# The LoRA-B products of the gate and up tiles, moved from behind the fourth chunk of x to behind the second and third

## The chip, the cores and the metric

The kernel runs on one core of a Trainium2 chip. The metric is the device time of one execution in microseconds (us). The core's engines are named as in the profile: PE (TensorE, matrix products), PEld (its weight loads), DVE (VectorE), ACT (ScalarE), POOL (GpSimd) and SP (SyncE, which issues most transfers). They run side by side and wait for one another on semaphores.

## The reference

Two residual layers on 8 x 128 tokens of 512 features. The first begins with a gated feed-forward block whose three weight matrices each have a low-rank correction (LoRA, rank 16), chosen for each batch by an index:

```
def lora_add(base, inp, A, B):
    t = einsum('bri,bni->bnr', A[idx], inp)
    return base + einsum('bor,bnr->bno', B[idx], t) * 0.5
gate = lora_add(x @ W_gate.T, x, A_gate, B_gate)      # 512 -> 1376
up   = lora_add(x @ W_up.T,   x, A_up,   B_up)
act  = silu(gate) * up
down = lora_add(act @ W_down.T, act, A_down, B_down)  # 1376 -> 512
```

A linear layer with eight averaged adapters follows and is added to x. The second layer is a linear layer with a batch's own sign matrix, then a mixture of 64 experts of rank 16, of which each token uses 16. All is float32. Only the products for `gate` and `up` are touched by the change.

## The kernel before

Each float32 operand is held as two parts, high and low, whose sum is the number to more digits than the PE takes in one pass. A product is made in three passes (`mm3`, lines 1150 to 1152: high by high, high by low, low by high). The x half is the moving operand, 512 tokens wide (`halves(s)`), and the weights are loaded into the array, 128 by 128.

The 1376 features of gate and up are cut into FT = 11 tiles of 128. Tiles 0, 1 and the last are done ahead, in code written out by hand. Tiles 2 to 9 run in a loop of four rounds with two tiles each (`pe.Fori`, line 1278). A tile is two halves of the tokens (s = 0, 1), and each half fills two banks of PSUM, one for gate (m = 0) and one for up (m = 1). So the loop fills 8 x 2 x 2 = 32 banks. For one bank the PE does:

- `project` (line 1157): for each of the four chunks of x (k = 0 to 3) three passes, 12 products of 512 columns;
- `adapt` (line 1168): two products of 256 columns that add the LoRA-B correction, one for each pair of batches (h = 0, 1). Their weights are `b_st`, 96 rows by 128 columns; the moving operand is `t_st`, 96 rows by 256 columns. The second one raises `gate_ready` or `up_ready`.

`b_st` holds the chosen B rows of the tile. POOL fetches them by an indirect transfer (line 416), ACT writes the high parts for all 96 rows (`b_high`, line 502, raises `b_hi`), and DVE then writes the low parts in rows 64 to 96 (`b_low`, line 789, raises `b_lo`). For w the same is done with `w_high` and `w_low`. The PE waits for `w_hi` and `w_lo` ahead of a tile (lines 1281 and 1282), and for `b_hi` and `b_lo` once in a tile, between `project` and `adapt` of its first bank (lines 1270 to 1272). Ahead of each bank it waits until ACT or DVE has emptied it. ACT and DVE turn the two banks of a half into a tile of `act` (silu, product, high and low part).

Just ahead of the loop stand the twelve LoRA-B products of three banks that were done ahead (`adapt_first(3)` to `(5)`). They free `b_st[0]`, which ACT and DVE then fill for tile 2, the loop's first. Just behind the loop stand the products with A of the down projection (line 1302), 22 of 256 columns in a row for each pair of batches.

The order on each engine is the order of the code; no scheduler moves anything.

Of the kernel before, what the change touches and what calls it, by code (L numbers as in the profile page):

```python
# [38 lines left out]
KD = D // P  # L39
HALF = T // 2  # L40
PAIR = 2 * SEQ
# [4 lines left out]
F_LAST = F - (FT - 1) * P  # L46
# [28 lines left out]
def build(nc, x_t, small_in, mask_w, w_gu, w_dn, a_gu, a_dn, b_three, b_gu, b_dn,  # L75
          lora_a, lora_b, w0_t, w1_t, bias1, wr_t, a_moe, b_moe, consts, out):
    with ExitStack() as ctx:
        base = -(-nc.sbuf_base // 32) * 32

        def sem(name):  # L80
            return ctx.enter_context(nc.semaphore(name))

        def at(name, shape, dtype, offset):
            return nc.alloc_sbuf_tensor_at(name, shape, dtype, offset=base + offset)
# [32 lines left out]
        def slots(name, shape, dtype, offset):  # L117
            return [at(f"{name}{u}", shape, dtype, R_U + 20 * KB * (1 - u) + offset) for u in range(2)]

        x_hl = at("x_hl", [P, 2, KD, T], F32R, R_X)  # L120
        w_hl = slots("w_hl", [P, 2, KD, 2, P], F32R, 0)
        w_raw = slots("w_raw", [P, KD, 2, P], F32, 8 * KB)
        b_raw = slots("b_raw", [P, NPAIR, 2, P], F32, 12 * KB)
        b_st = slots("b_st", [P, NPAIR, 2, P], F32R, 16 * KB)
        t_st = at("t_st", [P, NPAIR, 2, PAIR], F32R, R_T)
# [60 lines left out]
        ps = ctx.enter_context(nc.psum_tensor("ps", [P, 8, 512], F32))  # L186
# [27 lines left out]
        w_hi, w_lo, b_hi, b_lo = sem("w_hi"), sem("w_lo"), sem("b_hi"), sem("b_lo")  # L214
        t_ready, t_masked, t_hi, t_lo = sem("t_ready"), sem("t_masked"), sem("t_hi"), sem("t_lo")
        gate_ready, up_ready = sem("gate_ready"), sem("up_ready")
# [931 lines left out]
        def _(pe):  # L1148
            def mm3(out, w_high, w_low, m_high, m_low, start, stop):
                nc.tensor.matmul(out, w_high, m_high, start=start, stop=False)  # L1150
                nc.tensor.matmul(out, w_high, m_low, start=False, stop=False)  # L1151
                return nc.tensor.matmul(out, w_low, m_high, start=False, stop=stop)  # L1152

            def halves(s):
                return slice(s * HALF, s * HALF + HALF)

            def project(slot, bank, s, first=False, part=range(KD)):

                for k in part:
                    if first:  # L1160
                        pe.wait_ge(x_hi, KD * s + k + 1)
                        pe.wait_ge(x_lo, KD * s + k + 1)
                    m = bank % 2
                    last = mm3(ps[:, bank], w_hl[slot][:, 0, k, m], w_hl[slot][:, 1, k, m],
                               x_hl[:, 0, k, halves(s)], x_hl[:, 1, k, halves(s)], k == 0, False)
                return last

            def adapt(stack, bank, s, cols=P):

                m = bank % 2  # L1170
                for h in range(2):
                    last = nc.tensor.matmul(ps[0:cols, bank, h * PAIR:h * PAIR + PAIR],  # L1172
                                            stack[0:F_LAST, 2 * s + h, m, 0:cols], t_st[0:F_LAST, 2 * s + h, m],
                                            start=False, stop=h == 1, skip_group_check=cols < P)
                last.then_inc(up_ready if m else gate_ready, 1)
# [38 lines left out]
            def adapt_first(n):  # L1214
                f, s = FIRST_EVICTED[n]
                for m in range(2):
                    if f == LAST:
                        adapt(b_st[0], FIRST_BANK[n] + m, s, F_LAST)
                    else:
                        adapt(b_st[1] if f else b_other, FIRST_BANK[n] + m, s)  # L1220
# [24 lines left out]
            for k in range(KD):  # L1245
                for m in range(2):
                    last = project(0, FIRST_BANK[4] + m, 1, first=True, part=range(k, k + 1))
# [15 lines left out]
            for n in range(3, 6):  # L1263
                adapt_first(n)

            def tile_half(f, u, s):
                bank = 4 * (1 - u) + 2 * s
                pe.wait_ge(silu_done, 2 * f + s)
                project(u, bank, s)
                if s == 0:  # L1270
                    pe.wait_ge(b_hi, f - 1)
                    pe.wait_ge(b_lo, f - 1)
                adapt(b_st[u], bank, s)
                pe.wait_ge(glu_done, 2 * f + s)
                project(u, bank + 1, s)
                adapt(b_st[u], bank + 1, s)

            with pe.Fori(0, (FT - 3) // 2) as i:
                for u in range(2):
                    f = 2 * i + 2 + u  # L1280
                    pe.wait_ge(w_hi, W_FIRST + f - 1)
                    pe.wait_ge(w_lo, W_FIRST + f - 1)
                    for s in range(2):
                        tile_half(f, u, s)


            def act_part(f, h, lo, n):
                at0 = f * 2 * T + h * T + lo
                return act[:, at0:at0 + n]
# [5 lines left out]
            for p in range(NPAIR):  # L1295
                for f in by_eviction:
# [4 lines left out]
                    for h in range(2):  # L1301
                        last = nc.tensor.matmul(ps[:, 4 + p, 0:PAIR], stack,  # L1302
                                                act_part(f, h, p * PAIR, PAIR)[rows],
                                                start=(f == by_eviction[0] and h == 0),
                                                stop=(f == by_eviction[-1] and h == 1))
# [14 lines left out]
            for f in range(FT - 1):  # L1320
                pe.wait_ge(wd_hi, f + 1)
                pe.wait_ge(wd_lo, f + 1)
                for s in range(2):
# [5 lines left out]
                    for o in range(KD):  # L1329
                        cols = slice(o * P, o * P + P)  # L1330
                        last = mm3(ps[:, 4 * s + o], wd_hl[:, f % 2, 0, cols], wd_hl[:, f % 2, 1, cols],
                                   act_part(f, 0, s * HALF, HALF), act_part(f, 1, s * HALF, HALF), f == 0, False)
                last.then_inc(down_tiles, 1)

            for s in range(2):
# [4 lines left out]
                for o in range(KD):  # L1340
                    cols = slice(o * P, o * P + P)
                    for h in range(2):
                        p = 2 * s + h
                        last = mm3(ps[:, 4 * s + o, h * PAIR:h * PAIR + PAIR], last_hl[p][:, 0, cols], last_hl[p][:, 1, cols],
                                   act_part(FT - 1, 0, p * PAIR, PAIR), act_part(FT - 1, 1, p * PAIR, PAIR), False, h == 1)
# [5 lines left out]
            for s in range(2):  # L1351
                pe.wait_ge(d_lo, KD * s + KD)
                for o in range(KD):
                    cols = slice(o * P, o * P + P)
                    for k in range(KD):
                        last = mm3(ps[:, 4 * s + o], w0_hl[:, 0, k, cols], w0_hl[:, 1, k, cols],
                                   d_hl[:, 0, k, halves(s)], d_hl[:, 1, k, halves(s)], k == 0, k == KD - 1)
# [100 lines left out]
            for o in range(KD):  # L1458
                u = o % 2
# [95 lines left out]
```

## Time and profile before

| what | us |
|---|---|
| median of 3 runs | 356.58 (356.25 to 356.89) |
| the profiled execution | 356.68 |
| its span, first to last instruction | 355.0 |
| PE busy in the span | 351.1 (99%) |
| PEld busy | 298.3 (84%) |
| DVE busy | 200.2 (56%) |
| ACT busy | 143.6 (40%) |
| POOL busy | 79.5 (22%) |

Busy time of the PE is the time in which at least one product is in flight. A product's own duration (0.39 us for 512 columns) is longer than the distance from one start to the next, since the next starts while the one before still drains. What a product costs in a row of products is therefore read from the starts.

### The profile page before, as it was taken

What the parts mean: (1) busy time and instruction counts of PE and PEld (TensorE: products, weight loads), DVE (VectorE), ACT (ScalarE), POOL (GpSimd) and SP (SyncE); (2) the same over time, 40 slices, a digit from 0 to 9 for tenths busy, and PEclk for the clock granted to TensorE, in tenths of its full rate; (3) what the DMA queues carried; (4) which work ended last, traced back from release to release, by engine and by line L of the source; (5) the groups of instructions that cost most, each with busy time, mean ns of one, the idle gap of its engine ahead of it and who ended that gap; (6) DMA issues with size and microseconds to landing.
All of it is one profiled execution on the core that took longest, in us unless ns stands there. A gap on an engine that the chain in (4) does not pass through costs nothing.

```text
span 355.0 us, 4760 instructions
## 1 busy us (share of the span) xinstructions
PE 351.1 (99%) x1744; PEld 298.3 (84%) x1744; DVE 200.2 (56%) x299; ACT 143.6 (40%) x194; POOL 79.5 (22%) x86
## 2 busy tenths in 40 slices
PE   8999999999999999999999999999999999999996
PEld 8899888888888888988888898888888888888886
DVE  4787665525542543576583575689888868501101
ACT  5676554423442432454463561566362443201100
POOL 2460647885420003000000000000041154002200
PEclk9999999999999999999999999999999999999999
DMA  6962334132210043398219009110052012101011
GB/s 216 320 169 87 114 130 136 50 115 92 78 37 0 0 173 119 97 361 316 62 30 277 35 6 398 70 39 22 2 177 61 0 59 80 41 30 61 30 59 59
DMA packets 14802, 37.31 MB, mean 105 GB/s; under 512 B 2272, under 2 KB 4224, under 8 KB 13504
## 3 DMA queue, kind: packets, MB, share of 16 engines
q1 hardware_dynamic: 11920, 31.21, 25.5%
q0 software_dynamic: 2432, 5.57, 5.4%
q10 hardware_dynamic: 432, 0.30, 0.3%
q8 instruction: 11, 0.18, 0.2%
q14 instruction: 7, 0.06, 0.0%
HBM read 34.97 MB, written 2.10 MB: 104 GB/s over the span
## 4 chain that ended last, share of the span: by engine, by line
PE 99%; DVE 0%; issue 0%
PE ps L1150 29%; PE ps L1151 29%; PE ps L1152 29%; PE ps L1172 3%; PE ps L1302 3%; PE ps L1393 1%; PE ps L1380 1%; PE ps L1180 1%; PE ps L1187 1%; PE ps L1195 1%; PE ps L1191 1%; PE ps L1227 1%; PE ps L1402 0%; PE ps L1411 0%; DVE x L1143 0%
## 5 line engine op out<-in xcount | busy, mean ns | idle before, releaser
L1150 PE MATMUL ps<-x_hl,w_hl 128*128 128x512 f32 x144 | 56.5, 392 | 0.0
L1151 PE MATMUL ps<-x_hl,w_hl 128*128 128x512 f32 x144 | 56.4, 392 | 0.0
L1152 PE MATMUL ps<-x_hl,w_hl 128*128 128x512 f32 x144 | 56.0, 389 | 0.0
L461 POOL TENSOR_TENSOR am_hl<-am_raw,am_hl 128x512 fp32r<-128x512 f32 x8 | 11.0, 1387 | 136.8 <-ACT am_hl L478 136.8
L416 POOL DMA_INDIRECT b_raw<-b_gu,row_of x32 | 32.7, 1022 | 26.0 <-DVE b_st L777 17.8
L797 DVE TENSOR_TENSOR glu<-glu,ps 128x512 f32<-128x512 f32 (+1 forms) x22 | 15.0, 686 | 34.2 <-PE ps L1172 32.5
L478 ACT ACTIVATE act<-glu 128x512 f32 (+2 forms) x22 | 13.9, 631 | 47.6 <-DVE glu L797 44.4
L1152 PEld LDWEIGHTS ps<-x_hl,w_hl 128*128 128x128 f32 x144 | 27.0, 188 | 5.9
L1150 PEld LDWEIGHTS ps<-x_hl,w_hl 128*128 128x128 f32 x144 | 27.2, 189 | 4.8
L1150 PE MATMUL ps<-act,wd_hl 128*128 128x512 f32 x80 | 31.1, 389 | 0.0
L1151 PE MATMUL ps<-act,wd_hl 128*128 128x512 f32 x80 | 31.1, 389 | 0.0
L1152 PE MATMUL ps<-act,wd_hl 128*128 128x512 f32 x80 | 31.1, 389 | 0.0
L1151 PEld LDWEIGHTS ps<-x_hl,w_hl 128*128 128x128 f32 x144 | 27.2, 189 | 4.3
L1151 PE MATMUL ps<-hg,bm_hl 128*128 128x512 f32 (+1 forms) x72 | 26.3, 365 | 0.0
L1152 PE MATMUL ps<-hg,bm_hl 128*128 128x512 f32 (+1 forms) x72 | 26.3, 365 | 0.0
L1150 PE MATMUL ps<-hg,bm_hl 128*128 128x512 f32 (+1 forms) x72 | 26.3, 365 | 0.0
L1150 PE MATMUL ps<-c_hl,am_hl 128*128 128x512 f32 x64 | 25.3, 395 | 0.0
L1152 PE MATMUL ps<-c_hl,am_hl 128*128 128x512 f32 x64 | 25.0, 390 | 0.0
L1151 PE MATMUL ps<-c_hl,am_hl 128*128 128x512 f32 x64 | 24.9, 389 | 0.0
L777 DVE TENSOR_TENSOR act<-glu,act 128x512 f32 (+2 forms) x22 | 15.7, 718 | 16.3 <-ACT act L478 14.3
L984 DVE TENSOR_TENSOR wc_raw<-wc_raw,w_raw 128x2048 f32<-128x2048 f32 x8 | 18.3, 2291 | 8.9 <-ACT wc_raw L629 8.9
L1138 DVE TENSOR_TENSOR x<-ps,x 128x512 f32<-128x512 f32 x7 | 4.8, 691 | 31.8 <-PE ps L1152 31.8
(151 smaller groups left out, 741.5 us busy)
## 6 DMA issues: line engine op xcount, KB each, us to landing
wc_raw<-mask_w SPq DMA_DIRECT2D x8, 1024.0 KB, 7.4
w_raw<-w_gu SPq DMA_DIRECT2D x8, 512.0 KB
wd_raw<-w_dn SPq DMA_DIRECT2D x10, 256.0 KB
w_raw<-w_t SPq DMA_DIRECT2D x2, 1024.0 KB, 7.7
x<-x_t SPq DMA_DIRECT2D x2, 1024.0 KB, 6.7
am_raw<-a_moe SPq DMA_DIRECT2D x8, 256.0 KB, 2.6
bm_raw<-b_moe SPq DMA_DIRECT2D x4, 512.0 KB, 3.7
x_raw<-x_t SPq DMA_DIRECT2D x7, 256.0 KB, 5.1
```

The costliest lines, as they stand in the source:

```text
L416: nc.gpsimd.indirect_dma_start(b_raw[f % 2][0:F_LAST, p].rearrange("q m f -> q (m f)"), None, b_gu, bass.IndirectOffsetOnAxis(ap=row_of[0: ...
L461: nc.gpsimd.tensor_tensor(am_hl[:, j % AM_SLOTS, 1], am_raw[:, j % 2], am_hl[:, j % AM_SLOTS, 0].bitcast(F32), ALU.subtract).then_inc(am_l ...
L478: return nc.scalar.activation(out, in_, ACT.Copy)
L777: return nc.vector.tensor_tensor(out, whole, high.bitcast(F32), ALU.subtract)
L797: nc.vector.tensor_tensor(glu[rows, slot], glu[rows, slot], ps[rows, bank], ALU.mult).then_inc(glu_done, 1)
L984: nc.vector.tensor_tensor(wc[:], wc[:], w1_raw[:], ALU.add).then_inc(wc_added, 1)
L1138: nc.vector.tensor_tensor(x2[:, o, half], ps[:, 4 + n % 4], x2[:, o, half], ALU.add)\
L1150: nc.tensor.matmul(out, w_high, m_high, start=start, stop=False)
L1151: nc.tensor.matmul(out, w_high, m_low, start=False, stop=False)
L1152: return nc.tensor.matmul(out, w_low, m_high, start=False, stop=stop)
L1172: last = nc.tensor.matmul(ps[0:cols, bank, h * PAIR:h * PAIR + PAIR], stack[0:F_LAST, 2 * s + h, m, 0:cols], t_st[0:F_LAST, 2 * s + h, m], ...
L1302: last = nc.tensor.matmul(ps[:, 4 + p, 0:PAIR], stack, act_part(f, h, p * PAIR, PAIR)[rows], start=(f == by_eviction[0] and h == 0), stop= ...
```

## The change

The function `adapt` is no longer called in the loop. A new function, `project_adapted`, does the same 12 products of 512 columns and puts the two products of 256 columns between them: the one for h = 0 behind chunk k = 1, the one for h = 1 behind chunk k = 2. The last pass of chunk 3 ends the accumulation and raises the semaphore. The wait for `b_hi` and `b_lo` goes with the first LoRA-B product, behind chunk 1 of a tile's first bank. Number, sizes and operands of the products stay as they are, as do the code ahead of and behind the loop and all other engines.

```
+            def project_adapted(slot, bank, s, f=None):
+                m = bank % 2
+                for k in range(KD):
+                    last = mm3(ps[:, bank], w_hl[slot][:, 0, k, m], w_hl[slot][:, 1, k, m],
+                               x_hl[:, 0, k, halves(s)], x_hl[:, 1, k, halves(s)], k == 0, k == KD - 1)
+                    if k == 1 and f is not None:
+                        pe.wait_ge(b_hi, f - 1)
+                        pe.wait_ge(b_lo, f - 1)
+                    if k in (1, 2):
+                        h = k - 1
+                        nc.tensor.matmul(ps[:, bank, h * PAIR:h * PAIR + PAIR], b_st[slot][0:F_LAST, 2 * s + h, m],
+                                         t_st[0:F_LAST, 2 * s + h, m], start=False, stop=False)
+                last.then_inc(up_ready if m else gate_ready, 1)
+
             def tile_half(f, u, s):
                 bank = 4 * (1 - u) + 2 * s
                 pe.wait_ge(silu_done, 2 * f + s)
-                project(u, bank, s)
-                if s == 0:
-                    pe.wait_ge(b_hi, f - 1)
-                    pe.wait_ge(b_lo, f - 1)
-                adapt(b_st[u], bank, s)
+                project_adapted(u, bank, s, f if s == 0 else None)
                 pe.wait_ge(glu_done, 2 * f + s)
-                project(u, bank + 1, s)
-                adapt(b_st[u], bank + 1, s)
+                project_adapted(u, bank + 1, s)
```

First place, PE, the first bank of a tile (gate, s = 0), from the second half of `project` on. Before (`w_hl_59` and `b_st_65` are one slot of the weights and of the LoRA-B rows; L1172 is the line in `adapt`):

```order
L1150 MATMUL ps<-x_hl,w_hl_59 128x512
L1151 MATMUL ps<-x_hl,w_hl_59 128x512
L1152 MATMUL ps<-x_hl,w_hl_59 128x512
L1150 MATMUL ps<-x_hl,w_hl_59 128x512
L1151 MATMUL ps<-x_hl,w_hl_59 128x512
L1152 MATMUL ps<-x_hl,w_hl_59 128x512
L1271 REGISTER_ALU
L1172 MATMUL ps<-t_st,b_st_65 128x256 [waits b_lo,b_hi]
L1172 MATMUL ps<-t_st,b_st_65 128x256
L1150 MATMUL ps<-x_hl,w_hl_59 128x512 [waits glu_done]
```

The same place in the changed kernel, from the last product of chunk 0 to the next bank's first (L1277 is the product in `project_adapted`):

```order
L1152 MATMUL ps<-x_hl,w_hl_59 128x512
L1150 MATMUL ps<-x_hl,w_hl_59 128x512
L1151 MATMUL ps<-x_hl,w_hl_59 128x512
L1152 MATMUL ps<-x_hl,w_hl_59 128x512
L1273 REGISTER_ALU
L1277 MATMUL ps<-t_st,b_st_65 128x256 [waits b_lo,b_hi]
L1150 MATMUL ps<-x_hl,w_hl_59 128x512
L1151 MATMUL ps<-x_hl,w_hl_59 128x512
L1152 MATMUL ps<-x_hl,w_hl_59 128x512
L1277 MATMUL ps<-t_st,b_st_65 128x256
L1150 MATMUL ps<-x_hl,w_hl_59 128x512
L1151 MATMUL ps<-x_hl,w_hl_59 128x512
```

The product that waits for `b_lo` and `b_hi` moved from behind twelve products of 512 columns to behind six, and the six behind it now queue behind its wait. The two short products no longer touch: three long ones stand between them, and nine (three of this bank, six of the next) follow the second.

Second place, PE, the end of the loop's last bank and the first product behind the loop. Before:

```order
L1150 MATMUL ps<-x_hl,w_hl_60 128x512
L1151 MATMUL ps<-x_hl,w_hl_60 128x512
L1152 MATMUL ps<-x_hl,w_hl_60 128x512
L1172 MATMUL ps<-t_st,b_st_66 128x256 x2
L1278 REGISTER_ALU
L1278 COMPARE_AND_BRANCH
L1302 MATMUL ps<-act,ad_st 128x256 [waits act_hi,glu_done,act_lo,ad_lo,ad_hi]
```

And in the changed kernel (L1312 is what was L1302):

```order
L1277 MATMUL ps<-t_st,b_st_66 128x256
L1150 MATMUL ps<-x_hl,w_hl_60 128x512
L1151 MATMUL ps<-x_hl,w_hl_60 128x512
L1152 MATMUL ps<-x_hl,w_hl_60 128x512
L1288 REGISTER_ALU
L1288 COMPARE_AND_BRANCH
L1312 MATMUL ps<-act,ad_st 128x256 [waits act_hi,glu_done,act_lo,ad_lo,ad_hi]
```

Before, the loop ended in short products and short ones followed; now three long ones stand between the last LoRA-B product and those of line 1312.

## Rows read from the trace of the kernel before

**Rows 1.** The page: busy time of each engine; the chain that ended last.

```profile
PE 351.1 (99%) x1744; PEld 298.3 (84%) x1744; DVE 200.2 (56%) x299; ACT 143.6 (40%) x194; POOL 79.5 (22%) x86
...
PE 99%; DVE 0%; issue 0%
```

**Rows 2.** Waits of the PE over the whole span: all there are.

```profile
PE ps L1180 <- DVE warm L817: 1.2, 1, 1.2
```

**Rows 3.** The loop as one window: window, length, busy of PE, PEld, DVE, ACT, POOL, clock, DMA.

```profile
41.93:137.67 95.74, 95.74 (x452) 80.05 (x451) 45.46 (x56) 36.17 (x53) 38.62 (x48) 1.00 0.24 77
```

**Rows 4.** Timeline of the PE over one bank of the loop: start, duration, instruction.

```profile
98.44 0.40 PE L1172 MATMUL ps<-t_st,b_st 96*128 96x256 f32 x2
98.68 0.40 PE L1150 MATMUL ps<-x_hl,w_hl 128*128 128x512 f32 x1
98.91 0.40 PE L1151 MATMUL ps<-x_hl,w_hl 128*128 128x512 f32 x1
...
100.07 0.39 PE L1150 MATMUL ps<-x_hl,w_hl 128*128 128x512 f32 x1
...
101.43 0.40 PE L1172 MATMUL ps<-t_st,b_st 96*128 96x256 f32 x2
101.67 0.40 PE L1150 MATMUL ps<-x_hl,w_hl 128*128 128x512 f32 x1
```

**Rows 5.** Timeline of the PE behind the loop: short and long products by turns.

```profile
140.15 0.40 PE L1150 MATMUL ps<-lb_hl,la_hl 128*128 128x512 f32 x1
...
141.53 2.80 PE L1302 MATMUL ps<-act,ad_st 96*128 96x256 f32 x22
144.17 0.40 PE L1150 MATMUL ps<-lb_hl,la_hl 128*128 128x512 f32 x1
...
144.87 2.79 PE L1302 MATMUL ps<-act,ad_st 96*128 96x256 f32 x22
147.49 0.40 PE L1150 MATMUL ps<-lb_hl,la_hl 128*128 128x512 f32 x1
```

**Rows 6.** Timeline of the PE across the loop's start and in its first bank.

```profile
41.93 0.40 PE L1150 MATMUL ps<-x_hl,w_hl 128*128 128x512 f32 x1
...
43.09 0.39 PE L1152 MATMUL ps<-x_hl,w_hl 128*128 128x512 f32 x1
43.32 0.39 PE L1150 MATMUL ps<-x_hl,w_hl 128*128 128x512 f32 x1
...
44.68 0.40 PE L1172 MATMUL ps<-t_st,b_st 96*128 96x256 f32 x2
```

**Rows 7.** Timeline of DVE, with idle time before and its releaser: low parts of LoRA-B.

```profile
39.15 1.22 DVE L777 TENSOR_TENSOR t_st<-t_raw,t_st 32x1024 fp32r<-32x1024 f32 x1 [1.13 <-ACT t_st L478]
...
42.58 1.22 DVE L777 TENSOR_TENSOR b_st<-b_raw,b_st 32x1024 fp32r<-32x1024 f32 x1 [0.26 <-ACT b_st L478]
...
50.08 1.22 DVE L777 TENSOR_TENSOR b_st<-b_raw,b_st 32x1024 fp32r<-32x1024 f32 x1
...
59.16 1.22 DVE L777 TENSOR_TENSOR b_st<-b_raw,b_st 32x1024 fp32r<-32x1024 f32 x1 [1.35 <-ACT b_st L478]
...
117.57 1.22 DVE L777 TENSOR_TENSOR b_st<-b_raw,b_st 32x1024 fp32r<-32x1024 f32 x1
```

**Rows 8.** Timeline of the PE ahead of the loop: a product that waits for `t_st`.

```profile
40.05 0.39 PE L1152 MATMUL ps<-x_hl,w_hl 128*128 128x512 f32 x1
...
40.63 0.51 PE L1172 MATMUL ps<-t_st,b_st 96*96 96x256 f32 x3
```

**Rows 9.** Timeline of PEld there, and of ACT at the loop's start.

```profile
40.43 0.24 PEld L1172 LDWEIGHTS ps<-t_st,b_st 96*96 96x96 f32 x2 [0.41 <-issue]
...
41.50 1.05 ACT L478 ACTIVATE b_st<-b_raw 96x1024 fp32r<-96x1024 f32 x1
```

## The prediction, made before the changed kernel ran

> **What bounds the kernel now.** I read the page first. The PE is busy for 351.1 of 355.0 us, and the chain that ended last is 99% PE [rows 1]. The list of waits gives the PE just one, 1.2 us before its first product [rows 2]. In the loop, 41.93 to 137.67, it is busy for all 95.74 us at the full clock (2.4 GHz, shown as 1.00), while DVE is busy for 45.46 us and ACT for 36.17 [rows 3]. So whatever is added to the PE's stream of products is added to the end, and only what shortens that stream can gain. The 1.2 us aside, a wait of the PE is hidden by nothing, since no other engine sets the end.
>
> Next the timeline, since durations mislead here: a long product takes 0.39 us but the next one starts sooner. In a bank of the loop [rows 4] the reader should see three things. The last six products of 512 columns run from 100.07 to 101.43: 1.36 us, 0.227 each. The two LoRA-B products take 101.67 - 101.43 = 0.24, or 0.12 each. The first six long products, right behind a short pair, take 100.07 - 98.68 = 1.39 where six of the settled ones take 1.36. So a short pair costs its own 0.24 and some 0.03 more in the long ones behind it. I call that the toll. The exact loop agrees: 95.74 us / 32 = 2.992 us for a bank against 12 x 0.2267 + 0.24 = 2.960, a toll of 0.03 (rounded starts; taken as 0.027). Over 32 banks it is 0.86 us.
>
> **What the change does, part by part.** No product is added or removed, and none changes its size. Two things can move time: the place of the wait for `b_hi` and `b_lo`, and the neighbours of the short products.
>
> *The wait.* In the first bank of a tile the first LoRA-B product goes from behind 12 long ones to behind 6. In tile 2 the bank starts at 41.93 and the product behind the sixth starts at 43.32, where before the pair started at 44.68 [rows 6]: 1.36 us sooner. Its data comes from `b_low`, which DVE starts at 42.58 and ends 1.22 later, at 43.80 [rows 7]. Before, that was 0.88 ahead of the pair; now it is 0.48 behind the slot. Nothing makes DVE sooner: its operation waited for ACT's `b_high` [rows 7], which starts at 41.50 [rows 9], before the PE even enters the loop and so untouched by the change. The trace shows what such a release costs: the low part of `t_st` ended at 39.15 + 1.22 = 40.37 [rows 7], the weight load that waited for it began at 40.43 [rows 9] and the product behind the waiting one at 40.63 [rows 8], 0.26 behind the end of DVE's work. Here that gives 43.80 + 0.26 = 44.06 for the product behind the waiting one, and without a wait it would start at 43.32 + 0.12 = 43.44. The stall is 0.62. The load here has 128 columns and there it had 96, so I take 0.65. The floor is 43.80 - 43.32 = 0.48, as if release were instant; the ceiling 0.80, if the wait's own steps come on top (0.06 from 40.37 to 40.43 again, twice, and rounding). Behind the waiting product stand all of the PE's later products, and the PE's idle time is nowhere else for it to be absorbed [rows 2]. It goes to the end in full.
>
> The Trainium skill says of this, in "TensorE: Matmul & The Clock Gate", section "Part 3: Packing small matmuls — row/col tiling", that matmuls start and end strictly in program order and only weight loads may be pulled forward. By it the six long products behind the wait, whose operands are ready, can't pass it. The trace agrees: the first product behind the wait at 40.37 did not start before it.
>
> In the other tiles the wait is free. DVE ends `b_low` at 51.30 for tile 3, at 60.38 for tile 4 and at 118.79 for tile 9 [rows 7], while these tiles start at 41.93 + n x 11.97 (four banks of 2.992), that is 53.9, 65.9 and 125.7, and need it 1.4 us later. The nearest has 4 us of room.
>
> *The neighbours.* Before, a bank has one place where long products follow short ones, now it has two: three long ones behind the first LoRA-B product, nine behind the second. No row shows a single short product between long ones, so the toll of it must be bounded. Below: if one short product alone leaves no mark, the tolls vanish, -0.86. Rows behind the loop show two more things. The six long products at 140.15, behind a long run of short ones, take 141.53 - 140.15 = 1.38 [rows 5], so the toll is the same behind two short ones as behind 22: it saturates soon. And after three long products at 144.17 (0.70 for three, where 0.68 is the settled pace, a toll of 0.02), the 22 short ones take 147.49 - 144.87 = 2.62, where those at 141.53 take 2.64 [rows 5]: what three long ones lost, 22 short ones got back. So a toll of 0.02 that is cut off after three is not yet lost, and this is the neighbour that the first LoRA-B product gets. There are two ways to go on after one short product in that state. If it goes on where it stood, the nine long ones lose only the rest, and the bank's total stays at 0.027: no change. If a short product sets it back, the bank pays 0.018 for three, gets some 0.003 back in the short one and pays 0.027 again, 0.042 in all, 0.015 more than now: x 32 = +0.5 us. If a lone short product hurts more than a pair, say a full toll on each side without return (0.054 a bank), it is 0.027 x 32 = +0.86. I stand between the first two, at +0.2, since the recovery shown needs more than one short product but must not be none.
>
> A rule of the Trainium skill, same page, section "LDWEIGHTS (loading the stationary operand)", has a load of 128 columns last 128 / 1.2 = 107 ns whatever its rows. An estimate by that page: it fits beside a short product of 0.12, alone or in a pair, so the neighbours don't matter and only the wait counts. The trace agrees with the pitch of 0.12, but not with the 0.03 behind it [rows 4].
>
> *The rest.* `gate_ready` and `up_ready` are raised by a long product that starts 0.23 before the bank's end and lasts 0.39, in place of a short one that starts 0.12 before it and lasts 0.28: the same moment, 0.16 after. Behind the loop, three long products and then short ones stand where short ones followed short ones: by [rows 5] that is free. No transfer and no instruction of another engine moves.
>
> *The sum.* Against the profiled execution, 356.68 (355.0 of span and 1.7 around it): + 0.65 + 0.2 = 357.53. It lies 0.1 above the median of the runs; against the median, 356.58, it is 357.43, and I say 357.4.
>
> **The rivals.**
>
> - *The toll restarts with each short product* (chance 0.22, together with the still dearer lone one 0.29). For it: one pair already gives the whole toll, so one product may too. Against: in [rows 5] the loss was paid back. 356.58 + 0.65 + 0.5 = 357.7, in the dearer case 358.1.
> - *Only the wait counts* (0.18): the tolls stay as they are, as if carried on, or as by the skill's rule on loads. 357.2.
> - *The lone short product leaves little or no mark* (0.20): its weights are loaded beside a full long product, and the only short cover left is for the load behind it. Half the toll gone is 356.58 + 0.65 - 0.43 = 356.8; all gone is 356.4.
> - *Faster* (0.05): the tolls vanish and the wait costs nothing. Its place is tile 2, its price 0.86 saved, and it decides from the point where the stall is under 0.15 us: DVE would have to finish `b_low` by 43.3, 0.5 sooner than in [rows 7]. 355.7. Nothing in the rows lets DVE start sooner.
> - *The change doesn't do what it says*: excluded, as the order of the instructions shows both moves.
>
> **How the numbers follow.** My forecast, a wait of 0.65 with a slightly larger toll, has 0.28; the dearer tolls 0.29, the wait alone 0.18, less toll 0.20, faster 0.05. A difference of 0.2%, 0.71 us, is about what can be told from none here; so "slower" means above 357.29. The dearer tolls are above it (0.29), the forecast in six of seven cases (0.24), the wait alone in about a quarter, since its stall may be 0.8 (0.05): slower 0.58. Same: the rest of these and the smaller tolls, 0.37. Faster 0.05. The range: from 356.5, close to all tolls gone at the likely stall, to 358.2, the dearest tolls.
>
> **What would show it.** In the changed profile the PE should have a gap at about 43.4 us, in the loop's first bank and in no other, and the list of waits may name DVE's `b_st` or nothing. The low part should still end at 43.8, and everything from there to the end should be later by 0.65 plus the tolls. The tolls are read from a later bank, start to start: 2.99 us means no change, 2.96 that they vanished, 3.00 that they restart. The loop from 41.93 should take 96.4 to 96.9 us. I am wrong in kind if there is no gap in tile 2, if a bank's length changes by more than 0.03, or if the stages behind the loop change their length.

## The result, and the profile after

| | before | changed |
|---|---|---|
| median, 7 runs each | 356.39 us | 357.89 us |
| lowest to highest | 356.25 to 356.89 | 357.24 to 358.58 |
| profiled execution | 356.68 us | 357.88 us |
| its span | 355.0 us | 356.2 us |

The ratio is 1.0037, with a 95% interval of 1.0028 to 1.0047: the changed kernel is slower by about 1.3 us (1.0 to 1.7). The medians differ by 1.50, the profiled executions by 1.20 us. Three single executions of the experiments below took 715, 910 and 1252 us; they are left out of the ratios as slow.

The list of waits of the PE, which had one line before [rows 2], has three now. The columns are who waited for whom, us in total, times, longest:

```profile
PE ps L1180 <- DVE warm L817: 1.2, 1, 1.2
PE ps L1277 <- DVE b_st L777: 0.5, 1, 0.5
PE ps L1150 <- DVE w_last L777: 0.2, 1, 0.2
```

The second is the forecast one. The third lies ahead of the loop, in code that wasn't touched, and is absent when the same kernel runs again (below). It didn't cost much either, as the loop starts at 41.98 us against 41.93 before.

The first bank of the loop on the PE, to be set beside [rows 6]:

```profile
41.98 0.40 PE L1150 MATMUL ps<-x_hl,w_hl 128*128 128x512 f32 x1
...
43.14 0.39 PE L1152 MATMUL ps<-x_hl,w_hl 128*128 128x512 f32 x1
43.99 0.36 PE L1277 MATMUL ps<-t_st,b_st 96*128 96x256 f32 x1 [0.46 <-DVE b_st L777]
44.19 0.39 PE L1150 MATMUL ps<-x_hl,w_hl 128*128 128x512 f32 x1
```

DVE and the weight loads there, against [rows 7] and [rows 9]:

```profile
42.63 1.22 DVE L777 TENSOR_TENSOR b_st<-b_raw,b_st 32x1024 fp32r<-32x1024 f32 x1 [0.26 <-ACT b_st L478]
```

```profile
43.96 0.19 PEld L1277 LDWEIGHTS ps<-t_st,b_st 96*128 96x128 f32 x1 [0.86 <-issue]
```

Six long products start at 41.98, and the LoRA-B product's slot is 43.14 + 0.23 = 43.37. DVE ends `b_low` at 42.63 + 1.22 = 43.85, the weight load starts at 43.96, and the long product behind the waiting one at 44.19, where 43.37 + 0.12 = 43.49 would be its place. The stall is 0.70 us. The list shows only 0.46 of it, because it counts time in which no product is in flight, and the product ahead is in flight until 43.14 + 0.39 = 43.53.

A later bank, against [rows 4]:

```profile
98.06 0.28 PE L1277 MATMUL ps<-t_st,b_st 96*128 96x256 f32 x1
98.17 0.40 PE L1150 MATMUL ps<-x_hl,w_hl 128*128 128x512 f32 x1
98.41 0.40 PE L1151 MATMUL ps<-x_hl,w_hl 128*128 128x512 f32 x1
98.64 0.39 PE L1152 MATMUL ps<-x_hl,w_hl 128*128 128x512 f32 x1
98.87 0.28 PE L1277 MATMUL ps<-t_st,b_st 96*128 96x256 f32 x1
98.99 0.41 PE L1150 MATMUL ps<-x_hl,w_hl 128*128 128x512 f32 x1
99.23 0.40 PE L1151 MATMUL ps<-x_hl,w_hl 128*128 128x512 f32 x1
...
101.06 0.28 PE L1277 MATMUL ps<-t_st,b_st 96*128 96x256 f32 x1
```

From one first LoRA-B product to the next it is 101.06 - 98.06 = 3.00 us, against 101.43 - 98.44 = 2.99 [rows 4]; over many banks 3.000 against 2.987. The three long products behind the first take 98.87 - 98.17 = 0.70 where settled ones take 0.68: one short product alone leaves the same mark as a pair (by *mark* I mean the slower pace of the long products behind; the toll is what it costs). Behind the second short product the first long one takes 0.24, and all nine take 101.06 - 98.99 = 2.07 where nine settled ones take 2.04.

The loop and the stretch behind it as windows; the columns are those of [rows 3]:

```profile
41.98:138.70 96.72, 96.26 (x451) 79.94 (x449) 46.21 (x56) 36.16 (x53) 39.51 (x48) 1.00 0.23 76
138.70:152.00 13.30, 13.30 (x101) 12.78 (x100) 6.63 (x10) 5.00 (x8) 3.49 (x4) 1.00 0.49 140
```

The loop before runs to the start of the product behind its last pair:

```profile
137.51 2.80 PE L1302 MATMUL ps<-act,ad_st 96*128 96x256 f32 x22
```

The window of [rows 3] was 0.16 too long, so I take 137.51 - 41.93 = 95.58 for it (2.987 for a bank, where the prediction had 2.992). The loop is 96.72 - 95.58 = 1.14 us longer. That is all but 0.06 of the 1.20. Behind the loop nothing moved: from its end to the down projection's first product it is 13.30 in both.

### The profile page after: what moved, and what is told of

The parts are those of the page before. It is cut to its first block, busy times and chain, and to the rows that moved or that the text cites. A ratio compares the mean times of both kernels' runs of the same rounds, so it can differ in the third digit from the quotient of the medians.

```text
span 356.2 us, 4760 instructions
## 1 busy us (share of the span) xinstructions
PE 351.6 (99%) x1744; PEld 297.9 (84%) x1744; DVE 201.0 (56%) x299; ACT 143.6 (40%) x194; POOL 80.3 (23%) x86
## 4 chain that ended last, share of the span: by engine, by line
PE 94%; DMA 2%; SPq 1%; DVE 1%; ACT 1%; issue 0%; ACTq 0%
PE ps L1150 29%; PE ps L1151 28%; PE ps L1152 28%; PE ps L1312 3%; PE ps L1277 2%; DMA w_last_raw<-w_gu 2%; PE ps L1403 1%; PE ps L1390 1%; DVE w_last L777 1%; PE ps L1172 1%; PE ps L1412 0%; SPq L271 0%; DVE b_st L777 0%; ACT b_st L478 0%; PE ps L1421 0%
```

## The experiments

All times are against runs of the kernel before on the same chip. The loop's length in the profile is the sharper measure: it came out at 96.72 and 96.74 in two profiles of the changed kernel, while the loop's start wandered from 41.40 to 42.59 us over these profiles. In the code cuts `...` stands for lines left out.

**The changed kernel again** (no edit).

> The changed kernel once more, beside the others of this group on one chip. Theory (a wait of 0.70 us in tile 2's first bank, plus 0.0135 us more in each later bank because long products follow short ones twice): +1.1 us against before, with one gap of 0.6 to 0.7 us in the loop and a bank of 3.000 us. Rival (the medians of the first comparison, +1.50, hold something that the profiled execution, +1.20, doesn't show): +1.4 to +1.5, and the stretch ahead of the loop or behind it longer in the profile than before.

Ratio 1.003 (1.0018 to 1.0042), +1.1 us. The waits of the PE and the loop:

```profile
PE ps L1180 <- DVE warm L817: 1.2, 1, 1.2
PE ps L1277 <- DVE b_st L777: 0.5, 1, 0.5
```

```profile
41.40:138.14 96.74, 96.28 (x451) 79.83 (x449) 45.60 (x56) 36.17 (x53) 39.30 (x48) 1.00 0.24 76
```

The theory holds. The +1.5 between the first medians was the high end of what the comparison can tell; the interval of this one, 0.6 to 1.5 us, and that of the first, 1.0 to 1.7, both hold 1.14.

**The control: first round written out.**

A new function `tile` holds the two waits and the two halves of one tile, in the old order.

```
-            with pe.Fori(0, (FT - 3) // 2) as i:
...
+            for u in range(2):
+                tile(2 + u, u)
+            with pe.Fori(0, (FT - 5) // 2) as i:
                 for u in range(2):
...
+                    tile(2 * i + 4 + u, u)
```

> A control: the kernel before with the loop's first round (tiles 2 and 3) written out ahead of a loop of three rounds, products in the old order. Both theories: the same time as before within 0.1 us, a bank of 2.987 us, no wait. If it is slower by more than 0.2 us, the next kernel can't be read without it.

Ratio 1.001 (0.9997 to 1.0023), so no difference was told, though up to 0.8 us isn't excluded by the times alone. In the profile nothing is left for one: the loop went from 41.82 to 137.39, 95.57 us.

**The neighbours without the wait.**

In this kernel and the next three a function `fill` does the products of a bank. Its last argument names the chunks (0 to 3) behind which the LoRA-B products for h = 0 and h = 1 stand: (3, 3) is the old order, (1, 2) the changed one. A wait for `b_hi` and `b_lo` goes with h = 0.

```
+                first = (3, 3) if (f == 2 if isinstance(f, int) else False) and s == 0 else (1, 2)
...
+                fill(u, bank, s, f if s == 0 else None, first)
...
+                fill(u, bank + 1, s, None, (1, 2))
```

> The changed order in 31 of 32 banks; only tile 2's first bank keeps the pair behind the fourth chunk, so that the wait for b_lo has its old place there. Theory: no gap in the loop, 31 banks of 3.000 us, +0.4 us against before. Rival (the wait is the whole loss, the neighbours cost nothing on average): the same as before within 0.1 us.

Ratio 1.001 (1.0000 to 1.0019), +0.36 us. No wait of the PE in the loop, whose window is:

```profile
41.64:137.65 96.01, 96.01 (x450) 79.90 (x449) 45.37 (x56) 36.14 (x53) 38.69 (x48) 1.00 0.24 77
```

The loop is 0.43 us longer than before, 14 ns for each of 31 banks. The rival, that the neighbours cost nothing, falls by the profile; the times alone, whose interval begins at 1.0000, don't exclude it.

**The wait without the neighbours.**

The pair stands together, behind chunk 1.

```
+                fill(u, bank, s, f if s == 0 else None, (1, 1))
...
+                fill(u, bank + 1, s, None, (1, 1))
```

> The two LoRA-B products together, but behind the second chunk: the wait comes as early as in the changed kernel, and long products follow short ones only once in a bank. Theory: a gap of 0.6 to 0.7 us in tile 2's first bank and none later, banks of 2.987 us, +0.7 us against before. Rival (the neighbours are the whole loss and the wait is made good later): within 0.2 us of before.

Ratio 1.0025 (1.0016 to 1.0034), +0.9 us. The slot, and the loop:

```profile
42.74 0.39 PE L1152 MATMUL ps<-x_hl,w_hl 128*128 128x512 f32 x1
43.59 0.48 PE L1278 MATMUL ps<-t_st,b_st 96*128 96x256 f32 x2 [0.47 <-DVE b_st L777]
43.90 0.40 PE L1150 MATMUL ps<-x_hl,w_hl 128*128 128x512 f32 x1
```

```profile
41.58:137.90 96.32, 95.86 (x451) 79.74 (x449) 46.48 (x56) 36.15 (x53) 39.48 (x48) 1.00 0.25 77
```

The long product behind the pair has its place at 42.74 + 0.23 + 0.24 = 43.21 and starts at 43.90: a stall of 0.69 us. The loop is 0.74 us longer, with one gap. This and the 0.43 of the run before make 1.17, the whole change (1.14) within 0.03. The excess has a likely source: this kernel's loop ends in six long products where the loop before ended in a pair, so it holds one toll more. The two causes are separate and add up.

**Six long products on each side of a single one**, again without the wait.

```
+                first = (3, 3) if (f == 2 if isinstance(f, int) else False) and s == 0 else (1, 3)
...
+                fill(u, bank + 1, s, None, (1, 3))
```

> As the kernel of e3 (no wait in tile 2), but the two single LoRA-B products stand behind the second and the fourth chunk, with six long products on each side. Theory (a lone short product leaves the full mark on the long ones behind it, 0.027 us, and after six long ones nothing of it is given back): two full tolls a bank, 3.013 us, +0.8 us against before in 31 banks; dearer than e3 although the short products stand further apart. Rival (what costs is that short products stand close, with only three long ones between): less than e3, at or under +0.4 us.

Ratio 1.0032 (1.002 to 1.0044), +1.1 us (0.7 to 1.6). The loop:

```profile
41.88:138.28 96.40, 96.40 (x451) 79.96 (x449) 45.43 (x56) 36.16 (x53) 38.80 (x48) 1.00 0.24 77
```

It is 0.82 us longer, twice what three and nine long products between the short ones cost (0.43). Each LoRA-B product now draws a full toll: 0.82 / 31 = 0.026 more for each bank, one more toll. So distance doesn't help. With three between, the next short product comes before the mark has run its course, and the bank costs less.

**Single products behind the last two chunks.**

```
+                fill(u, bank, s, f if s == 0 else None, (2, 3))
...
+                fill(u, bank + 1, s, None, (2, 3))
```

> The changed order moved back by one chunk: single products behind the third and the fourth chunk, three long ones between and nine after, as in the changed kernel, but the wait for b_lo comes 0.68 us later. Theory (the stall is the distance from the slot to the end of DVE's work, plus the release): the slot in tile 2 is 2.07 us into the bank, some 0.2 after DVE's end, so the wait shrinks to 0 to 0.1 us; banks of 3.000 us; +0.4 to +0.5 us against before. Rival (the stall comes from putting a wait between long products at all, whenever it is met): +1.1 us as in e1.

Ratio 1.0021 (1.001 to 1.0031), +0.75 us (0.4 to 1.1). Its slot in tile 2, and the loop:

```profile
43.83 0.39 PE L1152 MATMUL ps<-x_hl,w_hl 128*128 128x512 f32 x1
44.06 0.30 PE L1278 MATMUL ps<-t_st,b_st 96*128 96x256 f32 x1
44.20 0.40 PE L1150 MATMUL ps<-x_hl,w_hl 128*128 128x512 f32 x1
```

```profile
41.99:138.02 96.03, 96.03 (x451) 79.86 (x449) 46.49 (x56) 36.19 (x53) 38.88 (x48) 1.00 0.25 77
```

DVE ends `b_low` at 43.86 in this profile. The product starts in its slot (43.83 + 0.23 = 44.06) and the next one 0.14 behind it in place of 0.12, so the stall has shrunk from 0.70 to 0.02. The loop is 0.45 longer, which is the neighbours' part alone. The stall comes from how far the slot lies ahead of DVE's end, and not from a wait standing between long products.

**Four together, and eight together.** The rows say that a toll is paid once for a run of short products of any length. So one kernel does both banks of a half first, then their four short products (`adapt_half`):

```
                 project(u, bank, s)
+                pe.wait_ge(glu_done, 2 * f + s)
+                project(u, bank + 1, s)
                 if s == 0:
                     pe.wait_ge(b_hi, f - 1)
                     pe.wait_ge(b_lo, f - 1)
-                adapt(b_st[u], bank, s)
-                pe.wait_ge(glu_done, 2 * f + s)
-                project(u, bank + 1, s)
-                adapt(b_st[u], bank + 1, s)
+                adapt_half(b_st[u], bank, s)
```

The other does all four banks of a tile, then their eight (`together` is 2, and 1 for the last tile):

```
+                    if s == 1 or together == 1:
+                        for t in ((0, 1) if together == 2 else (s,)):
+                            for m in range(2):
+                                adapt(b_st[u], 4 * (1 - u) + 2 * t + m, t)
```

> A version the toll points to: both banks of a half first, 24 long products, then their four LoRA-B products together. Theory: one toll in two banks, 0.0265 x 16 = 0.42 us less than before, no wait in tile 2 and none from the later gate_ready, since the bank isn't needed again for eight banks. Rival (the toll grows with the number of short products in a row, or ACT's later start holds up the PE): no gain, a longer toll in the timeline or a gap.

> The same for a whole tile: 48 long products, then eight short ones; the last tile by halves as in e7, so that its first half is ready for the products behind the loop. Theory: 9 tolls instead of 32, 23 x 0.0265 = 0.6 us less than before. Rival: ACT and DVE get two halves at once and the tile's end holds up the next one's banks or weights, a gap in the loop.

Four: ratio 0.9997 (0.9985 to 1.0009). Eight: 0.9993 (0.9984 to 1.0001). No difference told, but the loops are shorter and without a gap:

```profile
42.13:137.28 95.15, 95.15 (x451) 79.81 (x449) 46.58 (x56) 36.50 (x52) 38.90 (x48) 1.00 0.25 78
```

```profile
41.83:136.79 94.96, 94.96 (x450) 79.78 (x449) 44.50 (x56) 35.85 (x52) 39.48 (x48) 1.00 0.25 78
```

The loop is 0.43 us shorter for 16 tolls saved and 0.62 shorter for 23, 0.027 each as worked out. The times were too loose to tell, so the shorter one ran again:

> The kernel of e8 once more, for its time alone: its profile had a loop 0.61 us shorter than before, its runs a ratio of 0.9993 (0.9984 to 1.0001). Theory: -0.6 us, ratio 0.9983. Rival (the gain in the loop is given back in executions that aren't profiled): a ratio at 1.000.

Ratio 0.9982 (0.997 to 0.9994), 355.97 against 356.65 us, with a loop of 94.96 again. By these runs this version is about 0.6 us faster than the kernel before. That is small, and the first of its two comparisons alone doesn't show it. Against the changed kernel its loop is 96.72 - 94.96 = 1.76 us shorter.

**What leaves the mark.** In place of the pair stands one product of 512 columns, in a function `adapt_wide` called where `adapt` was. It leaves out the second pair's own LoRA-B weights.

```
+                last = nc.tensor.matmul(ps[:, bank], stack[0:F_LAST, 2 * s, m], t_st[0:F_LAST, 2 * s:2 * s + 2, m],
+                                        start=False, stop=True)
```

> Order as before, but in place of the two LoRA-B products of 256 columns one product of 512 columns and still 96 rows stands at the bank's end; it takes the weights of the first pair of batches for both, so the second pair's own LoRA-B weights are left out. Theory (the toll comes from the short width alone): 13 products at the long pace, a bank of 13 x 0.2267 = 2.947 us and no slower long products behind it; 32 x 0.040 = 1.28 us less than before. Rival (the mark comes from the 96 rows, or from going to other tensors): the long products behind it start 233, 236, 228 ns apart as before, a bank of 2.973 us, 0.4 us less than before.

Ratio 0.9987 (0.9974 to 1.0), -0.5 us. The PE at its first bank's end:

```profile
45.34 0.40 PE L1269 MATMUL ps<-t_st,b_st 96*128 96x512 f32 x1
45.57 0.40 PE L1150 MATMUL ps<-x_hl,w_hl 128*128 128x512 f32 x1
45.81 0.40 PE L1151 MATMUL ps<-x_hl,w_hl 128*128 128x512 f32 x1
...
46.27 0.39 PE L1150 MATMUL ps<-x_hl,w_hl 128*128 128x512 f32 x1
```

My theory, that the toll comes from the short width alone, fell. A product as wide as its neighbours leaves a mark too: the four from 45.34 take 0.93 us where settled ones take 0.91, and the loop is 95.16 long, not 94.3. The steps aren't the same, though. The wide product itself and the three behind it start 233, 237, 233 and 231 ns apart, where behind a pair five long ones do (233, 236, 228, 233 and 231); the sum over the settled 227 is 27 ns in both. This product differs from its neighbours in its 96 rows, in a moving operand of two separate pieces and in the tensors it reads. Two more kernels, which ran once each beside a single run of the kernel before, part the first two. Both leave out the LoRA-B correction of these tiles. With 96 rows in one piece:

```
+                last = nc.tensor.matmul(ps[:, bank], stack[0:F_LAST, 2 * s, m], x_hl[0:F_LAST, 0, 0, halves(s)],
+                                        start=False, stop=True)
```

With two pieces in 128 rows:

```
+                last = nc.tensor.matmul(ps[:, bank], w_hl[slot][:, 0, 0, m],
+                                        x_hl[:, 0, 0:2, s * HALF:s * HALF + PAIR],
+                                        start=False, stop=True)
```

> As e9, but the moving operand of the one wide product is an unbroken row of 512 elements of x in 96 rows, in place of two pieces of 256 of t_st; the LoRA-B correction of these tiles is left out. If the mark comes from the 96 rows: 233, 237 and 233 ns between starts as in e9 and a loop of 95.15 us. If it comes from the broken row of the moving operand: the long pace of 227 ns throughout and a loop of 94.3 us.

> The other half: the one wide product reads two pieces of 256 elements of x in all 128 rows, with weights of w_hl in 128 rows; the LoRA-B correction of these tiles is left out. If the mark comes from the 96 rows: the long pace of 227 ns throughout and a loop of 94.3 us. If it comes from the broken row: a mark as in e9 and a loop of 95.15 us.

Their times were 356.03 and 355.67 us against 357.26, one execution each, from which nothing is told. The loop with 96 rows, and with 128:

```profile
41.69:136.84 95.15, 95.15 (x418) 78.27 (x417) 45.53 (x56) 36.16 (x53) 38.51 (x48) 1.00 0.25 78
```

```profile
42.14:136.46 94.32, 94.32 (x419) 78.08 (x417) 45.67 (x56) 36.17 (x53) 38.32 (x48) 1.00 0.25 78
```

The kernel with 96 rows at full width pays the whole toll, the one with two pieces in 128 rows none (32 x 13 products at 0.2267 are 94.3). The two also differ in where the weights come from, `b_st` or `w_hl`, which no kernel here parts from the rows. The trace of the kernel before speaks against that as the cause. There the long products go over to other tensors in both operands at 308.29, with 128 rows throughout, and keep the settled pace:

```profile
308.07 0.39 PE L1152 MATMUL ps<-c_hl,am_hl 128*128 128x512 f32 x1
308.29 0.39 PE L1150 MATMUL ps<-hg,bm_hl 128*128 128x512 f32 x1
...
308.97 0.39 PE L1150 MATMUL ps<-hg,bm_hl 128*128 128x512 f32 x1
```

The three from 308.29 take 0.68. But rows aren't the only way to a mark. Before the loop of the kernel before, products with 128 rows and 256 columns are followed by long ones, and the mark is there:

```profile
22.05 0.28 PE L1152 MATMUL ps<-x_hl,w_last 128*128 128x256 f32 x1
22.17 0.40 PE L1150 MATMUL ps<-x_hl,w_hl 128*128 128x512 f32 x1
22.40 0.40 PE L1151 MATMUL ps<-x_hl,w_hl 128*128 128x512 f32 x1
22.64 0.39 PE L1152 MATMUL ps<-x_hl,w_hl 128*128 128x512 f32 x1
22.86 0.40 PE L1150 MATMUL ps<-x_hl,w_hl 128*128 128x512 f32 x1
```

The first three take 22.86 - 22.17 = 0.69, with the same unequal steps as in [rows 4]. So narrow products leave a mark with all 128 rows, and products with fewer rows leave one at full width. What happens inside the PE stays open, as no run here shows it.

## Why the prediction was right, and where it was off

The direction, slower by more than 0.2%, came out, and the time of 357.89 us is in the range. The forecast of +0.85 was too small by 0.3 against the profile (+1.14 in the loop) and by some 0.45 against the ratio of the times (+1.3). That "slower" came out is partly luck: the wait alone, at 0.70 us, doesn't pass the 0.71 (0.2%) that I had set for it, and the part that carried it over, the neighbours, was argued wrongly. Point by point:

- *The wait* was the main term, 0.65 with bounds of 0.48 and 0.80; it measured 0.70. It is in tile 2's first bank, nowhere else, and goes to the end in full. The place, the releaser and the cause were right, and moving the slot by one chunk took all but 0.02 of it away. The size was off by 0.05 to 0.08 in the release: from DVE's end to the weight load it took 0.11 us here, where the row I took it from had 0.06, and to the product behind the waiting one 0.34 in place of 0.26. Why it is longer wasn't tried.
- *The neighbours* were the mis-sized term. I put +0.2 between "no change" and "restart with +0.5"; the runs showed 0.43. The argument for a value in the middle was that the mark isn't lost while it is cut off after three long products. That was half right: it is why three and nine cost 0.43 and six and six cost 0.82. But the short product behind the three gave back next to nothing, and the long ones behind it paid in full again. Averaged over the loop's banks, three long ones take 0.698 us for a settled 0.680, the short one behind them 0.117 for 0.120, and the nine 2.067 for 2.040. That makes 0.018 - 0.003 + 0.027 = 0.042 a bank, which is the rival's sum; I had set against it a recovery that 22 short products showed, and one gives only 0.003 of it. The rival "the toll restarts", 357.7, was the right case in kind; its +15 ns a bank was measured as +14. I gave it 0.22 and my own middle 0.28.
- *Only the wait counts*, where the neighbours are indifferent, and *less toll* are out: the kernel with the neighbours alone was 0.43 longer in its loop. With the first falls the estimate that rested on the Trainium skill ("TensorE: Matmul & The Clock Gate", section "LDWEIGHTS (loading the stationary operand)"), that a weight load fits beside a short product and the order is therefore free. The trace has loads beside products of 0.12 us throughout, and the order still costs. A load's record is 0.19 us long here, as at 43.96, where the Trainium skill's figure there is 107 ns; the records of neighbouring loads overlap.
- *What a toll is* was wrong. I tied it to the width of the product. For this kernel's sum that made no difference, since nothing in it changed width or rows; but the wide product with 96 rows was forecast wrong by it, with -1.28 us where its loop shows -0.42.
- *The rest* held: semaphores raised by the long product move nothing, and the stretch behind the loop kept its 13.30 us.

The two parts make up the 1.14 within 0.03 us. The times add a scatter that the loop doesn't have. In the profiles it sits ahead of the loop, whose start moved by up to 1.2 us; why it moves wasn't tried.

## What to carry to other kernels

Where one engine is busy all the time, a wait moved forward costs the time by which its slot is ahead of the data, plus the release. So look at the first round of a loop: it is fed by the code ahead, and can have less room than the rounds behind it. Here, at the new place, the data of tile 2 came 0.48 us too late, while the nearest other tile has 4 us of room. In these kernels the short products were cheapest in one run and dear when scattered, because the stream paid up to 27 ns each time it returned to long ones. And when a trace shows a small cost behind every group of odd ones, take the mark apart by width, rows and layout before building on a cause; the cause seen first may be one of two, as here.

## What the runs showed of the hardware that I had not expected

- After products of 256 columns, the next five of 512 columns with 128 rows start 233, 236, 228, 233 and 231 ns apart where settled ones start 227 apart: 27 ns in all, about 18 of it in the first three. It is the same after one, two, four, eight or 22 of them. (The row of 22 in [rows 5] merges two with 96 rows and 20 with 128.)
- A product of 512 columns with 96 rows costs the same 27 ns over the settled pace, spread over itself and the three behind it.
- A product of 512 columns over two separate pieces of SBUF in 128 rows runs at the settled pace, 227 ns, and leaves no mark (one profile).
- A product that waited for DVE lets the one behind it start 0.34 us after DVE's end here and 0.26 in [rows 8]; the list of waits shows only the part in which nothing is in flight, 0.46 of a stall of 0.70.
